# Attention's key tails: 122 and 32 keys for 128 and 26, high and low tails of one pair stacked in 128 rows

## What is computed

```python
q, k, v = heads(ln(x) @ Wq + bq), heads(ctx @ Wk + bk), heads(ctx @ Wv + bv)   # 16 heads of 64, 154 keys
p = softmax(where(mask, -1e30, q @ k.T / 8))
x = x + merge(p @ v) @ Wo + bo
logits = ln2(ln(x)) @ ln3(slot_embeds).T                   # 1024 tokens x 16 experts x 64 slots
slots = softmax(logits, tokens).T @ ln2(ln(x))
eout = (gelu(slots @ Wg + bg) * (slots @ Wu + bu)) @ Wd + bd
x = x + softmax(logits, all_slots) @ eout
```

## Time and profile before

| | before |
|---|---|
| median of 3 runs | 576.8 us (575.91 to 577.07) |
| the profiled execution | 577.03 us, span 575.3 us |
| TensorE matmul, busy | 542.2 us (94%), 3880 matmuls |
| VectorE, busy | 461.4 us (80%) |
| ScalarE, busy | 395.4 us (69%) |
| GpSimd, busy | 312.7 us (54%) |

### The profile page before, as it was taken

The page is one execution under the profiler, slowest core; times in us unless marked ns, Lnnn a source line. Parts: engine busy times, 40 slices in busy tenths (PEclk is TensorE's granted clock), DMA queues, the critical chain, the costliest instruction groups (busy, mean ns, idle before and its releaser), DMA issues.

```text
span 575.3 us, 11921 instructions
## 1 busy us (share of the span) xinstructions
PE 542.2 (94%) x3880; PEld 502.7 (87%) x3880; DVE 461.4 (80%) x1352; ACT 395.4 (69%) x1070; POOL 312.7 (54%) x329
## 2 busy tenths in 40 slices
PE   5889999999999999999989998899979999999998
PEld 3778999999999989999978876799957888899997
DVE  5788778789787979889676998887778999985553
ACT  3786969789695959779563545678877676736652
POOL 7364645454545354544356656877387999920000
PEclk9899999999999999999999999899999999999999
DMA  8602000000020000000001433050268888515552
GB/s 210 217 2 74 2 2 2 1 2 1 2 93 2 2 2 1 2 0 3 2 1 75 171 159 148 36 189 3 72 200 285 279 273 278 186 38 177 169 169 73
DMA packets 34940, 51.78 MB, mean 90 GB/s; under 512 B 6109, under 2 KB 21409, under 8 KB 34881
## 3 DMA queue, kind: packets, MB, share of 16 engines
q1 hardware_dynamic: 34881, 51.04, 26.8%
HBM read 40.54 MB, written 10.49 MB: 89 GB/s over the span
## 4 chain that ended last, share of the span: by engine, by line
PE 58%; DVE 18%; POOL 9%; ACT 7%; issue 6%; DMA 2%; SPq 0%; DVEq 0%; POOLq 0%; ACTq 0%
PE ps L1391 8%; PE ps L1452 8%; PE ps L1257 7%; PE ps L1342 6%; DVE w_gu_low L925 5%; PE ps L1323 5%; PE ps L1375 5%; PE ps L1354 4%; PE ps L1377 3%; POOL prob L639 2%; PE ps L1511 2%; PE ps L1423 2%; ACT expo L775 2%; DVE colmax L1127 2%; DVE eo_high L1204 1%
## 5 line engine op out<-in xcount | busy, mean ns | idle before, releaser
L639 POOL TENSOR_TENSOR prob<-expo,prec 128x512 f32<-128x512 f32 x64 | 66.9, 1045 | 97.3 <-DVE prec L1041 96.0
L775 ACT ACTIVATE expo<-expo,nmin 128x154 f32<-128x154 f32 x256 | 106.7, 425 | 4.2 <-DVE nmin L1030 4.1
L1030 DVE CUSTOM_DVE_ANT_0 expo<-ps,maskb 128x154 f32<-128x154 f32 x256 | 69.2, 314 | 11.7 <-PE ps L1342 11.0
L1342 PE MATMUL ps<-kbd,qT_high 128*128 128x308 f32 x256 | 61.0, 322 | 0.3 <-ACT qT_high L711 0.3
L1050 DVE TENSOR_TENSOR pT_low<-ps,pT_high 128x512 fp32r<-128x512 f32 (+1 forms) x96 | 57.5, 599 | 4.3 <-ACT pT_high L789 3.8
L789 ACT CAST pT_high<-ps 128x512 fp32r<-128x512 f32 (+1 forms) x96 | 49.2, 515 | 15.3 <-PE ps L1354 11.6
L711 ACT ACTIVATE oT_high<-ps,bv_c 128x256 fp32r<-128x256 f32 x64 | 30.0, 469 | 36.7 <-PE ps L1377 36.7
L696 POOL TENSOR_TENSOR w_gu_low<-w_raw,w_gu_high 128x1024 fp32r<-128x1024 f32 x18 | 45.2, 2515 | 13.7 <-ACT w_gu_high L733 13.7
L775 ACT ACTIVATION_READ_ACCUMULATOR expo<-expo,nmin 128x1 f32 x256 | 50.8, 198 | 0.0
L696 POOL TENSOR_TENSOR wkq_low<-w_raw,wkq_high 128x1024 fp32r<-128x1024 f32 x14 | 45.6, 3259 | 2.4 <-ACT wkq_high L733 2.4
L925 DVE TENSOR_TENSOR w_gu_low<-w_raw,w_gu_high 128x1024 fp32r<-128x1024 f32 x15 | 40.1, 2676 | 3.7 <-ACT w_gu_high L733 3.7
(11 more groups left out here) (222 smaller groups left out, 1772.3 us busy)
## 6 DMA issues: line engine op xcount, KB each, us to landing
logits_dram<-lsb SPq DMA_DIRECT2D x16, 512.0 KB, 2.6
w_raw<-in_L_ffn_Wg_dram SPq DMA_DIRECT2D x16, 512.0 KB, 4.3
w_raw<-in_L_ffn_Wu_dram SPq DMA_DIRECT2D x16, 512.0 KB, 4.5
w_raw<-in_L_ffn_Wd_dram SPq DMA_DIRECT2D x16, 512.0 KB, 4.1
lraw<-logits_dram SPq DMA_DIRECT2D x13, 512.0 KB, 3.7
out_dram<-gate SPq DMA_DIRECT2D x16, 128.0 KB, 1.7
x<-in_x_dram SPq DMA_DIRECT2D x1, 1792.0 KB, 13.3
wk_raw<-in_L_xattn_Wk_dram SPq DMA_DIRECT2D x2, 512.0 KB, 5.1
```

The source lines that it names most:

```text
L639: pool.tensor_tensor(prob[:, n % 2, :, heads, :], expo[:, n % 2, pp, :, :, 0:P], prec[:, n % 2, pp].unsqueeze(3).to_broadcast([P, 2, 2, P] ...
L775: ins = act.activation(row, row, ACT.Exp, scale=-1.0, bias=nmin[:, n % 2, pp, j, h:h + 1], accum_out=psums[:, n % 2, pp, j, h:h + 1])
L1030: ins = dve.tensor_tensor_reduce(out=expo[:, n % 2, pp, j, h, :], in0=ps[:, s % NS, h * SK:(h + 1) * SK], in1=maskb[:, (2 * (n // QUADS) + ...
L1342: ins = pe.matmul(dst, qT[s][:, n % 2, pp, j * P:(j + 1) * P], kbd[:, b, m, p, :], start=(r == 0), stop=(r == 2))
```

## The change

The keys are divided 122 and 32 instead of 128 and 26. The tail now has 4 x 32 = 128 rows for the four heads of a quad, 64 for each pair. For a pair `pp`, ScalarE writes the high halves of its 64 tail rows into the same partitions of a new tile `pTt[:, n % 2, pp]`, and VectorE writes the low halves into the other 64 partitions of that tile. So one tile holds high rows over low rows of one pair. `vt_high` has the values for both halves, since the copies of the tail context fill all 128 rows and `quad_mask` lets a head's values through in the rows of both pairs; `vt_low` is zero in the rows that meet low rows of the probabilities. One matmul with `vt_high` gives high x high and low x high, one with `vt_low` gives high x low: two tail matmuls a pair instead of three, `PV` eight instead of nine. The tail cast and the tail subtraction become two instructions each, over 64 partitions, and `VL` two as well. Two counting semaphores become one for each part (`zeros_ready`, `split_low`). `quad_mask` is made by five clears instead of one and two selects, and `vt_low` is cleared by VectorE at the start.

```diff
@@ -167,14 +167,15 @@
-    TAIL = SK - P
+    TAIL = P // 4
+    MAIN = SK - TAIL
+    REST = SK - P
...
-    T4 = 4 * TAIL
...
-    assert D == 2 * P and DM == 1024 and ES == 1024 and F == 512 and B == 2 and T4 <= P
+    assert D == 2 * P and DM == 1024 and ES == 1024 and F == 512 and B == 2 and TAIL <= SK <= P + TAIL
@@ -308,7 +309,8 @@
-    vt = halves(att, "vt", [T4, B, QUADS, 4 * DH])
+    vt_high = sb(att, "vt_high", [P, B, QUADS, 4 * DH], F32R)
+    vt_low = sb(att, "vt_low", [P, B, QUADS, 4 * DH], F32R)
@@ -321,20 +323,21 @@
-    prob = sb(att, "prob", [P, 2, 2, 4, P])
+    prob = sb(att, "prob", [P, 2, 2, 4, MAIN])
...
-    ctx_tail = sb(pro, "ctx_tail", [TAIL, B, D])
+    ctx_tail = sb(pro, "ctx_tail", [REST, B, D])
...
-    v_f = sb(pro, "v_f", [T4, 2, 4 * DH])
-    quad_mask = sb(pro, "quad_mask", [T4, 4, DH])
+    v_f = sb(pro, "v_f", [P, 2, 4 * DH])
+    quad_mask = sb(pro, "quad_mask", [P, 4, DH])
...
-    pT = halves(loop, "pT", [P, 2, 5, 2 * P])
+    pT = halves(loop, "pT", [P, 2, 4, 2 * P])
+    pTt = sb(loop, "pT_tail", [P, 2, 2, 2 * P], F32R)
@@ -599,19 +603,18 @@
-                pool.engine_nop().then_inc(zeros_ready, 1)
+                pool.engine_nop().then_inc(zeros_ready[ev[1]], 1)
...
-                    link(pool.memset(quad_mask[:], 1.0))
-                    link(pool.affine_select(out=quad_mask[:], in_=quad_mask[:], compare_op=ALU.is_ge, fill=0.0, base=0,
-                                            pattern=[[-TAIL, 4], [0, DH]], channel_multiplier=1))
-                    pool.affine_select(out=quad_mask[:], in_=quad_mask[:], compare_op=ALU.is_ge, fill=0.0,
-                                       base=TAIL - 1, pattern=[[TAIL, 4], [0, DH]], channel_multiplier=-1)\
-                        .then_inc(const_pool, 1)
+                    link(pool.memset(quad_mask[:], 0.0))
+                    for a in range(4):
...
+                        link(pool.memset(quad_mask[a * TAIL:(a + 1) * TAIL, a % 2::2, :], 1.0))
+                    pool.engine_nop().then_inc(const_pool, 1)
...
-                pool.tensor_tensor(low, raw, high, ALU.subtract).then_inc(split_low[i], 1)
+                pool.tensor_tensor(low, raw, high, ALU.subtract).then_inc(split_low[i][c], 1)
@@ -636,9 +639,9 @@
-                pool.tensor_tensor(prob[:, n % 2, :, heads, :], expo[:, n % 2, pp, :, :, 0:P],
-                                   prec[:, n % 2, pp].unsqueeze(3).to_broadcast([P, 2, 2, P]), ALU.mult)
-                pool.tensor_tensor(prob_t[:, n % 2, :, heads, :], expo[:, n % 2, pp, :, :, P:SK],
+                pool.tensor_tensor(prob[:, n % 2, :, heads, :], expo[:, n % 2, pp, :, :, 0:MAIN],
+                                   prec[:, n % 2, pp].unsqueeze(3).to_broadcast([P, 2, 2, MAIN]), ALU.mult)
+                pool.tensor_tensor(prob_t[:, n % 2, :, heads, :], expo[:, n % 2, pp, :, :, MAIN:SK],
@@ -785,10 +788,15 @@
                     wait_done(act, ("PV", n - 2, 1))
-                rows, tiles = (P, 2) if t < 2 else (T4, 1)
-                act.copy(pT[0][0:rows, n % 2, 2 * t:2 * t + tiles],
-                         ps[0:rows, NS + k % NT, 0:tiles * 2 * P].rearrange("p (t n) -> p t n", t=tiles))\
-                    .then_inc(t_high, 1)
+                src = ps[:, NS + k % NT, :].rearrange("p (t n) -> p t n", t=2)
+                if t < 2:
+                    ins = act.copy(pT[0][0:MAIN, n % 2, 2 * t:2 * t + 2], src[0:MAIN])
+                else:
...
+                    for pp in range(2):
+                        own = slice(64 * pp, 64 * pp + 64)
+                        ins = act.copy(pTt[own, n % 2, pp], src[own, 0])
+                ins.then_inc(t_high, 1)
             elif ev[0] == "PV":
                 _, n, pp = ev
@@ -927,7 +935,11 @@
-                .then_inc(vm_zeros, 1)
+                .then_inc(v_zeros, 1)
+        for pp in range(2):
...
+            dve.memset(vt_low[64 - 64 * pp:P - 64 * pp, :, :, pp * P:(pp + 1) * P].rearrange("p b q n -> p (b q) n")
+                       .bitcast(F32), 0.0).then_inc(v_zeros, 1)
@@ -939,7 +951,7 @@
-                                              cT[s][:, kk, :, P:SK].unsqueeze(2).to_broadcast([P, B, 4, TAIL]))
+                                              cT[s][:, kk, :, MAIN:SK].unsqueeze(2).to_broadcast([P, B, 4, TAIL]))
@@ -979,16 +991,19 @@
-                    dve.tensor_tensor(v_f[:], acc(no)[0:T4, :].rearrange("p (q n) -> p q n", q=2),
-                                      quad_mask[:].rearrange("p a d -> p (a d)").unsqueeze(1).to_broadcast([T4, 2, 4 * DH]),
+                    dve.tensor_tensor(v_f[:], acc(no).rearrange("p (q n) -> p q n", q=2),
+                                      quad_mask[:].rearrange("p a d -> p (a d)").unsqueeze(1).to_broadcast([P, 2, 4 * DH]),
...
-                dve.wait_ge(vt_high, tail_no[tail] + 1)
-                dve.tensor_tensor(vt[1][:, b, 2 * c:2 * c + 2, :], v_f[:], vt[0][:, b, 2 * c:2 * c + 2, :],
-                                  ALU.subtract).then_inc(v_low, 1)
+                dve.wait_ge(vt_rounded, tail_no[tail] + 1)
+                for pp in range(2):
+                    own, cols = slice(64 * pp, 64 * pp + 64), slice(pp * P, (pp + 1) * P)
+                    ins = dve.tensor_tensor(vt_low[own, b, 2 * c:2 * c + 2, cols], v_f[own, :, cols],
+                                            vt_high[own, b, 2 * c:2 * c + 2, cols], ALU.subtract)
+                ins.then_inc(v_low, 1)
@@ -1046,10 +1061,16 @@
                     keys_over(dve)
-                rows, tiles = (P, 2) if t < 2 else (T4, 1)
-                dve.tensor_tensor(pT[1][0:rows, n % 2, 2 * t:2 * t + tiles],
-                                  ps[0:rows, NS + k % NT, 0:tiles * 2 * P].rearrange("p (t n) -> p t n", t=tiles),
-                                  pT[0][0:rows, n % 2, 2 * t:2 * t + tiles], ALU.subtract).then_inc(t_free, 1)
+                src = ps[:, NS + k % NT, :].rearrange("p (t n) -> p t n", t=2)
+                if t < 2:
+                    tiles = (slice(0, MAIN), n % 2, slice(2 * t, 2 * t + 2))
+                    ins = dve.tensor_tensor(pT[1][tiles], src[0:MAIN], pT[0][tiles], ALU.subtract)
+                else:
...
+                    for pp in range(2):
+                        own, other = slice(64 * pp, 64 * pp + 64), slice(64 - 64 * pp, P - 64 * pp)
+                        ins = dve.tensor_tensor(pTt[other, n % 2, pp], src[own, 0], pTt[own, n % 2, pp], ALU.subtract)
+                ins.then_inc(t_free, 1)
             elif ev[0] == "PV":
                 _, n, pp = ev
@@ -1362,20 +1383,21 @@
                 b, p = 2 * g // TB, 2 * q + pp
                 dst = bank(ev)
-                both = max(t_no["T", n, pp], t_no["T", n, 2]) + 1
-                pe.wait_ge(t_high, both)
+                pe.wait_ge(t_high, t_no["T", n, pp] + 1)
                 if n == 0:
                     pe.wait_ge(v_low, 2 * B)
-                    pe.wait_ge(vm_zeros, 2)
+                    pe.wait_ge(v_zeros, 4)
                     wait_used(pe, LAST_V)
                 for r, (s, m) in enumerate(PASSES):
                     if m == 1:
-                        pe.wait_ge(t_free, both)
+                        pe.wait_ge(t_free, t_no["T", n, pp] + 1)
                     for h in range(2):
-                        pe.matmul(dst[:, 0:2 * P], vm[s][:, b, p, h * DH:h * DH + P], pT[m][:, n % 2, 2 * pp + h],
-                                  start=(r == 0 and h == 0), stop=False)
-                    ins = pe.matmul(dst[:, 0:2 * P], vt[s][:, b, q, pp * P:(pp + 1) * P], pT[m][0:T4, n % 2, 4],
-                                    start=False, stop=(r == 2))
+                        pe.matmul(dst[:, 0:2 * P], vm[s][0:MAIN, b, p, h * DH:h * DH + P],
+                                  pT[m][0:MAIN, n % 2, 2 * pp + h], start=(r == 0 and h == 0), stop=False)
+                pe.wait_ge(t_free, t_no["T", n, 2] + 1)
+                for v in (vt_high, vt_low):
+                    ins = pe.matmul(dst[:, 0:2 * P], v[:, b, q, pp * P:(pp + 1) * P], pTt[:, n % 2, pp],
+                                    start=False, stop=(v is vt_low))
                 ins.then_inc(acc_full, 1)
             elif ev[0] == "Y":
...
```

More of the change, by code:

```diff
@@ L970, in step @@
                 if t == 0:
[L971 to L972 removed]
+                    src = acc(no)[0:MAIN].rearrange("p (q a d) -> p q a d", q=4, a=2)
+                    view = [v[0:MAIN, b, 4 * c:4 * c + 4, :].rearrange("p q (a d) -> p q a d", a=3)[:, :, 0:3:2] for v in vm]
                     dve.wait_ge(v_high, v_no[ev] + 1)
```

42 lines of the change are left out of this document (21 added, 21 removed).

## The result

The changed kernel takes 586.85 us (median of 4, 584.56 to 587.34) against 576.62 (575.91 to 577.07) for the kernel before: ratio 1.0173, 95% interval 1.0151 to 1.0196. It is slower, as forecast, but by 10.2 us where 4.4 was forecast, and the median lies above the stated range of 575.0 to 585.0. The profiled execution took 586.73 us, span 584.8.

What follows compares the result with a forecast made beforehand. TensorE leads by a few tenths of a microsecond, ScalarE and VectorE nearly full in the loop. Terms 0.25 + 0.3 - 0.6 + 1.0 + 2.9 + 0.6 = +4.45 on 577.03 gave 581.5, 581.2 against the median; range 575.0 to 585.0.

Steps and rivals of the forecast that it cites:

- What it removes: Attention loop, per step and pair: one of nine `PV` matmuls, 0.12 us each, 64 in all, 7.7 us.
- What costs nothing: GpSimd's new shapes (-0.04 and +0.04 us), transposes, `vt_low` clears, quadrant mask and split semaphores were all taken as covered.
- 0.66 us a step on VectorE, 0.52 on ScalarE: Loop's tail subtraction and cast, as two 64-partition halves without overlap: extra 0.66 us a step on VectorE, 0.52 on ScalarE.
- The second rival: Loop tails: the pair loses its overlap, the neighbours don't; extras 0.43 and 0.40 us, about +1, 577.8 us; chance 16%.
- The first: Rival: TensorE's saving comes through in light steps (no result projection), others lagging within buffers; 569.1 or 571.0 us; chance 14%.
- The late part, +1.0 and +2.9: 180 to 206 us: VectorE late, TensorE waiting, +1.0; two cycles from 213 to 266 us: 1.45 each, +2.9.
- One sign of being right: TensorE's stall near 206 us would be a microsecond longer.
- The early cycles, 3 x -0.2: Three four-step cycles up to 180 us: TensorE early by 0.45 less ScalarE's 0.25, so -0.2 each, -0.6 together.
- The third rival: ScalarE and VectorE both set light steps everywhere: 6.64 us for 6.4, about +8 in all, 585 us; chance 10%.
- Start, 50.5 to 83, drain: 0.25 + 0.3 + 0.6: Start, `vt_low` in halves: +0.25; 50.5 to 83 us, one tail cast on the path: +0.3; drain, 278 to 300: +0.6.

Runs made afterwards that it cites:

- nine: The changed kernel with a third tail matmul that repeats the second, so nine matmuls a pair again, halves kept: 586.19 us, ratio 1.0170.
- keys_divided: The kernel before with the keys divided 122 and 32 and nothing else: 576.58 us, ratio 1.0006.
- whole_tiles: The changed kernel without the stacking: tail cast and subtraction once each over 128 partitions, still eight matmuls a pair, result differs: 573.75 us, ratio 0.9946.
- dve_halves: Like `whole_tiles`, but VectorE's tail subtraction as two of 64 partitions that write to the other 64; ScalarE's cast whole: 583.08 us, ratio 1.0102.
- act_halves: Like `whole_tiles`, but ScalarE's tail cast as two of 64 partitions; VectorE's subtraction whole: 578.78 us, ratio 1.0035.
- late_tail: The changed kernel with VectorE's pair of tail subtractions queued behind the minima of the next score bank: 583.97 us, ratio 1.0136.
- filled_three: The changed kernel with `VL` as one instruction over 128 partitions and added matmuls filling three TensorE waits: 583.73 us, ratio 1.0139.

## Why the prediction was wrong in size and right in sign

- *What it removes*: 64 matmuls at 0.12 us, right as a count and a rate, and right that they would not come through. They are worth 2.6 us with whole tiles and nothing with the halves (`nine`).
- *What costs nothing*: held. `keys_divided` shows it as a whole for the division of the keys, GpSimd by its rows (-43 and +34 ns).
- *0.66 us a step on VectorE, 0.52 on ScalarE*: measured 0.69 and 0.43. The earlier trace rows were the right rows. On ScalarE the first half keeps the overlap with its predecessor (130.67 is before 129.96 + 0.84), which the sum had taken away. The second rival, in which the neighbours keep their overlap, is out on VectorE, but came nearer on ScalarE (0.40 us). The first is out too: the late cycles stretched.
- *The late part, +1.0 and +2.9*: measured +1.19 and +3.13. The reasoning from 0.35 us of free VectorE time and no slack at `T2` was right: `T2` waits for `prob_t` again at 230.68 and 237.50, where TensorE in the kernel before had no idle time from 220 to 234 us. One sign of being right did not show as stated: TensorE's stall near 206 us grew from 1.32 to 1.52 us, not by a microsecond; steps 17, 18 and 19 grew by 0.43, 0.16 and 0.61.
- *The early cycles, 3 x -0.2*: **this step failed.** Measured +0.95 in steps 4 to 15. The first light step of a cycle does gain its 0.24 (6.14 for 6.38), but the second gives it back (6.59) and the step with `Y` loses 0.17 (12.31 for 12.14): about +0.15 a cycle for the -0.2 of the sum. The sum let ScalarE fall behind by 0.25 and compared that with a slack of 0.45 at `Y`; it left VectorE out, with 11.08 of 12.80 us busy. With both engines whole (`whole_tiles`) the same two steps are 6.16 and 11.85; `dve_halves` alone shows 6.62 and 12.30, `act_halves` alone 6.45 and 12.12. So each engine's halves alone undo the gain, and VectorE's by themselves give the whole loss. The pair, 0.9 us of VectorE, stands in front of the minima on which exponentials and score banks wait, so VectorE's tail lay on the path although the engine had 1.7 us free. `late_tail` shows that for the step with `Y` and for the late cycles; what sets the second light step is not settled. The third rival's light step, 6.64, was near for every second one; its total doesn't follow from its own terms (4.45 + 0.6 + 3.8 gives +8.9, not about 8). In addition step 15, which I counted as early, already carries the first of the slot embeddings' normalisation (from 168.9 us in the kernel before): 12.82 for 12.14, 0.5 more than its sisters.
- *Start, 50.5 to 83, drain: 0.25 + 0.3 + 0.6*: **this failed too**, 1.15 forecast, 4.2 measured. What was left out, a term put at nothing, is TensorE's clock. The change lengthens two waits of 1.31 us to 2.10 and 1.83; behind each TensorE stood at 1.2 GHz, and step 0 took 8.17 us for 6.90. With the waits filled the loop is back to +0.51 in steps 0 to 3 and +0.84 in steps 28 to 30, and all four rows together are at +0.9. A smaller part is the start itself: 0.7 us for 0.25, since VectorE's first pairs of tail subtractions come on top of `VL`. The times of the single executions agree: the one of 584.56 us had a mean granted clock of 0.997, the other three (586.73 to 587.34) 0.988. That one is still 7.9 us above the kernel before, so the clock is the smaller part of the whole loss.
- By the table, 1.5 us of the 5.0 that were missing is the early cycles, 0.4 the late terms, 3.1 the start, the first steps and the drain. Against a changed kernel without half-clock stretches in the loop (`filled_three`, span +6.1) the sum of +4.45 is 1.6 short, nearly all of it (1.5) the early cycles.

## What to carry to other kernels

In these runs splitting an elementwise instruction by partitions cost more than the second instruction: count every change of start partition, of inputs or output, in it and in the one behind it (here 0.11 to 0.12 us each on VectorE, for instructions of 256 elements a partition), and keep runs of such instructions on one start partition. An engine's free time over a stretch says little about one long item that stands in front of work others wait for: look at what is queued behind it. And where a change lengthens a wait of TensorE to the lengths behind which the clock fell here (7 of 21 at 1.52 to 1.95 us, 4 of 4 at 2.00 to 2.13), add the clock to the sum as a chance, and read the mean granted clock of every execution before comparing medians.
